# Quantised layer: maxima over partitions by a TensorE product; slot lists laid out by tile

## What is computed

```python
x = x + tanh(g_xattn[0]) * L0_xattn(layernorm(x), ctx)      # linear mix with the mean of the context
x = x + tanh(g_ffn[0])   * L0_ffn(layernorm(x))             # quantised layer
x = x + tanh(g_xattn[1]) * L1_xattn(layernorm(x), ctx)
x = x + tanh(g_ffn[1])   * L1_ffn(layernorm(x))             # 8 experts, the best two of each token
x = x + ...                                                  # layers 2 and 3
```

```python
def act_qdq(x):
    scale = max(max(abs(x)) / 32767, 1e-12)
    return clip(round(x / scale), -32768, 32767) * scale
x = act_qdq(x); up = act_qdq(x @ Wup.T); gate = act_qdq(x @ Wgate.T)
gate = act_qdq(gate * round_u16(sigmoid(gate)))
out = act_qdq(gate * up) @ Wdown.T
```

## Time and profile before

| | us |
|---|---|
| median of 3 runs | 1646.64 |
| lowest, highest | 1642.23, 1647.51 |
| profiled execution, its own time | 1650.74 |
| its span (first to last instruction) | 1649.0 |
| busy: PE, DVE, POOL, ACT | 1249.0, 1018.0, 857.6, 785.8 |
| mean granted TensorE clock | 0.878 |

### The profile page before, as it was taken

One profiled execution on the slowest core, in us unless ns is written; L12 is line 12 of the kernel. 1 busy time (PEld: TensorE's weight loads), 2 busy tenths in 40 slices (PEclk: granted clock), 3 DMA queues, 4 the chain that ended last, 5 costly groups with the idle time before them and its releaser, 6 DMA issues. The chain is left out here.

```text
span 1649.0 us, 27008 instructions
## 1 busy us (share of the span) xinstructions
PE 1249.0 (76%) x9879; PEld 859.6 (52%) x9880; DVE 1018.0 (62%) x2196; ACT 785.8 (48%) x1473; POOL 857.6 (52%) x1040
## 2 busy tenths in 40 slices
PE   4482658999547999565999958679998684999994
PEld 4231535555426899354555525545555553566663
DVE  5589748998461111354899967768886488544421
ACT  2277436777413444254667746556666341222220
POOL 5200046666305553584555549656665343588875
PEclk9696879999757999786899979889999597899997
DMA  2000000000025887110000000000000003344442
GB/s 100 7 0 0 1 2 2 2 2 1 4 58 165 246 228 201 48 52 21 1 2 2 2 15 1 1 3 2 2 1 1 11 31 127 75 97 97 98 87 24
DMA packets 51796, 74.96 MB, mean 45 GB/s; under 512 B 8169, under 2 KB 31602, under 8 KB 51282
## 3 DMA queue, kind: packets, MB, share of 16 engines
q1 hardware_dynamic: 35858, 55.01, 10.5%
q0 software_dynamic: 15808, 18.24, 6.7%
HBM read 57.09 MB, written 16.12 MB: 44 GB/s over the span
## 5 line engine op out<-in xcount | busy, mean ns | idle before, releaser
L1506 PE MATMUL ps<-topk_up_sb,topk_wu 128*128 128x512 f32 x256 | 118.7, 608 | 0.7 <-ACT topk_up_sb L1400 0.7
L500 POOL TENSOR_TENSOR l3x_prob<-l3x_prob,l3x_rden 128x1232 f32<-128x1232 f32 x32 | 71.9, 2248 | 78.3 <-DVE l3x_rden L633 78.3
L500 POOL TENSOR_TENSOR l2x_prob<-l2x_prob,l2x_rden 128x1232 f32<-128x1232 f32 x32 | 71.9, 2248 | 74.7 <-DVE l2x_rden L633 74.7
L1330 POOL DMA_INDIRECT out<-topk_shared,l3f_route_slots x64 | 100.2, 1565 | 17.5 <-issue 17.5
L1407 ACT ACTIVATE topk_ga<-ps 128x512 f32<-128x512 f32 x64 | 38.3, 598 | 148.0 <-PE ps L1506 148.0
L594 ACT ACTIVATE l3x_pt<-ps 77x512 f32<-77x512 f32 x128 | 72.5, 591 | 71.4 <-PE ps L544 71.4
L1626 DVE TENSOR_TENSOR sb_xnT<-topk_ga,ps 128x512 f32<-128x512 f32 x64 | 44.0, 687 | 97.8 <-ACT topk_ga L1407 97.8
L500 POOL TENSOR_TENSOR l1x_prob<-l1x_prob,l1x_rden 128x1232 f32<-128x1232 f32 x32 | 71.9, 2248 | 57.6 <-DVE l1x_rden L633 57.6
L1980 DVE TENSOR_TENSOR l1f_g_y<-ps,l1f_g_wd 128x256 f32<-128x256 f32 x39 | 16.6, 425 | 137.6 <-PE ps L1923 137.6
L1950 ACT ACTIVATE l1f_g_h<-ps,l1f_g_wd 128x256 f32<-128x256 f32 x156 | 63.5, 475 | 74.2 <-DMA l1f_g_wd<-l1f_W 41.0
L594 ACT ACTIVATE l2x_pt<-ps 77x512 f32<-77x512 f32 x128 | 72.7, 591 | 55.0 <-PE ps L544 55.0
(11 more groups left out here) (499 smaller groups left out, 3490.9 us busy)
## 6 DMA issues: line engine op xcount, KB each, us to landing
l1f_g_wd<-l1f_W SPq DMA_DIRECT2D x39, 322.0 KB, 4.0
l1f_g_wu<-l1f_W SPq DMA_DIRECT2D x39, 256.0 KB, 3.8
topk_wu<-l3f_W SPq DMA_DIRECT2D x16, 512.0 KB, 3.8
l1f_y_rows<-l1f_g_y SPq DMA_DIRECT2D x39, 128.0 KB, 4.0
topk_wd<-l3f_W SPq DMA_DIRECT2D x16, 256.0 KB, 2.7
l3f_rows<-l3f_route_own_rows SPq DMA_DIRECT2D x1, 2304.0 KB, 8.0
sb_x<-x SPq DMA_DIRECT2D x1, 2048.0 KB, 7.5
l1f_rows<-l1f_route_own_rows SPq DMA_DIRECT2D x1, 2048.0 KB, 9.2
```

The lines of the kernel that those rows point to most:

```text
L500: pool.tensor_tensor(prob[n % 4][:], prob[n % 4][:], rden[n % 2][:].unsqueeze(2).broadcast_to([P, HEADS, KEYS]), ALU.mult).then_inc(normed, 1)
L1330: pool.indirect_dma_start(out=out_rows, out_offset=spot(g, i), in_=y[g % 2][:, i, :], in_offset=None, compute_op=ALU.add).then_inc(y_added ...
L1506: ins = pe.matmul(ps[:, 2 * (c % 2) + i, :], wu[g % W][:, (i * CX + c) * P:(i * CX + c + 1) * P], xgT[g % 2][:], start=True, stop=True)
```

## The change

1. GpSimd no longer exchanges maxima. TensorE multiplies the column own maximum, spread over 128 columns as weights, with the identity: row by row the result in bank 6 is the list of all 128 partitions' maxima. VectorE's new `highest` reduces these 128 numbers from PSUM (semaphore found). The exchange run on `magic` goes too.
2. In slot_lists the tables hi_hot, hi_num, hi_table are laid out [P, CH, NHI], tile first. The tile number gets a full table (tile_table) and hi a spread copy (hi_wide[p]), both written by ScalarE, and hi_16 goes. The six instructions for the experts stand behind high(1).

```diff
@@ -722,13 +724,18 @@
 
+            def highest(k, n):
+                v.wait_ge(all_max, n)
+                v.tensor_reduce(col(k, 1), ps[:, 6, 0:P], X, ALU.max).then_inc(found, 1)
+                v.wait_ge(found, n)
+
             def own_scale(k, n):
-                v.wait_ge(all_max, n)
+                highest(k, n)
                 step(v.tensor_scalar(col(k, 2), col(k, 1), 1.0 / QMAX, 1e-12, ALU.mult, ALU.max))
...
             def product_scale(k, n):
-                v.wait_ge(all_max, n)
+                highest(k, n)
                 step(v.tensor_scalar(col(k, 2), col(k, 1), col(k, 5), 1e-12, ALU.mult, ALU.max))
@@ -839,20 +846,9 @@
         def _(pool):
-            def everywhere(k, n):
-                pool.wait_ge(own_max, n)
-                pool.partition_all_reduce(col(k, 1), col(k, 0), P, RMAX).then_inc(all_max, 1)
-
             pool.memset(magic[:], -MAGIC).then_inc(magic_ready, 1)
-            pool.wait_ge(magic_ready, 1)
-            pool.partition_all_reduce(qs[:, 31:32], magic[:], P, RMAX).then_inc(warm, 1)
             for b in range(NBLK):
                 norm.centre(pool, "pool", b)
-            everywhere(XS, 1)
-            everywhere(GATE, 2)
-            everywhere(UP, 3)
-            everywhere(H, 4)
-            everywhere(O, 5)
 
@@ -927,6 +923,13 @@
 
+            def everywhere(k, n):
+                pe.wait_ge(own_max, n)
+                if n >= 2:
+                    pe.wait_ge(found, n - 1)
+                pe.matmul(ps[:, 6, 0:P], col(k, 0).broadcast_to([P, P]), t["ident"][:], start=True, stop=True).then_inc(all_max, 1)
+
+            everywhere(XS, 1)
             for j in range(NBLK):
@@ -938,7 +941,12 @@
                 product(0, j).then_inc(up_made, 1)
+                if j == 0:
+                    everywhere(GATE, 2)
+            everywhere(UP, 3)
+            everywhere(H, 4)
             pe.wait_ge(loads, 32)
+            pe.wait_ge(found, 4)
             for b in range(NBLK):
@@ -950,6 +958,8 @@
                 ins.then_inc(vl_made, 1)
+            pe.wait_ge(kl_kept, NK)
+            everywhere(O, 5)
             for b in range(NBLK):
@@ -1694,8 +1704,9 @@
         lo_table, lo_16 = sb("lo_table", [P, P, CH], BF16), sb("lo_16", [P, NC * CH], BF16)
-        hi_hot, hi_num = [sb(f"hi_hot{p}", [P, NHI, CH], BF16) for p in range(2)], [sb(f"hi_num{p}", [P, 2, NHI, CH], BF16) for p in range(2)]
-        hi_table, hi_16, tile_16 = sb("hi_table", [P, NHI, CH], BF16), sb("hi_16", [P, NC * CH], BF16), sb("tile_16", [P, CH], BF16)
+        hi_hot, hi_num = [sb(f"hi_hot{p}", [P, CH, NHI], BF16) for p in range(2)], [sb(f"hi_num{p}", [P, CH, 2, NHI], BF16) for p in range(2)]
+        hi_table, tile_table = sb("hi_table", [P, CH, NHI], BF16), sb("tile_table", [P, CH, NHI], BF16)
+        hi_wide, hi_spread, hi_found = [sb(f"hi_wide{p}", [P, CH, NHI], BF16) for p in range(2)], s.one("hi_spread"), s.one("hi_found")
         nums = sb("nums", [P, NG * G, 2])
@@ -1743,8 +1754,11 @@
             sc.wait_ge(iotas, 6)
-            sc.activation(hi_table[:], iota_hi[:].unsqueeze(2).broadcast_to([P, NHI, CH]), ACT.Copy).then_inc(table_ready, 1)
-            sc.activation(tile_16[:], tile[:], ACT.Copy).then_inc(table_ready, 1)
+            sc.activation(hi_table[:], iota_hi[:].unsqueeze(1).broadcast_to([P, CH, NHI]), ACT.Copy).then_inc(table_ready, 1)
+            sc.activation(tile_table[:], tile[:].unsqueeze(2).broadcast_to([P, CH, NHI]), ACT.Copy).then_inc(table_ready, 1)
+            for p in range(2):
+                sc.wait_ge(hi_found, 1)
+                sc.activation(hi_wide[p][:], hi[:, p * CH:(p + 1) * CH].unsqueeze(2).broadcast_to([P, CH, NHI]), ACT.Copy).then_inc(hi_spread, 1)
             take(0, 1)
@@ -1756,7 +1770,7 @@
                 for i in range(CH):
-                    ins = pe.matmul(ps[:, 4, 0:2 * NHI], lo_hot[p][:, :, i], hi_num[p][:, :, :, i].rearrange("p k h -> p (k h)"),
+                    ins = pe.matmul(ps[:, 4, 0:2 * NHI], lo_hot[p][:, :, i], hi_num[p][:, i, :, :].rearrange("p k h -> p (k h)"),
                                     start=(p == 0 and i == 0), stop=(p == 1 and i == CH - 1))
@@ -1775,13 +1789,6 @@
                 step(v.tensor_tensor(first[:], first[:], groups[:], ALU.subtract))
-                step(v.memset(begun[:], 0.0))
-                step(v.tensor_tensor(begun[:, :, 0:E], iota_g[:].unsqueeze(2).broadcast_to([P, NG, E]),
-                                     first[:].unsqueeze(1).broadcast_to([P, NG, E]), ALU.is_ge))
-                step(v.tensor_tensor(u["of_expert"][:], begun[:, :, 0:E], begun[:, :, 1:E + 1], ALU.subtract))
-                step(v.tensor_tensor(begun[:, :, 0:E], u["of_expert"][:], iota_e[:].unsqueeze(1).broadcast_to([P, NG, E]), ALU.mult))
-                step(v.tensor_reduce(eid[:], begun[:, :, 0:E], X, ALU.add))
-                step(v.tensor_copy(u["expert_of"][:], eid[:]))
             step(v.tensor_tensor(flat(rank), flat(rank), ps[:, 2, 0:W], ALU.subtract))
@@ -1791,8 +1798,8 @@
             step(v.tensor_scalar(hi[:], lo[:], 1.0 / P, -0.5 + 0.5 / P, ALU.mult, ALU.add))
-            step(v.tensor_scalar(hi[:], hi[:], MAGIC, MAGIC, ALU.add, ALU.subtract))
-            step(v.tensor_copy(hi_16[:], hi[:]))
+            v.tensor_scalar(hi[:], hi[:], MAGIC, MAGIC, ALU.add, ALU.subtract).then_inc(hi_found, 1)
+            v.wait_ge(hi_found, 1)
             step(v.scalar_tensor_tensor(lo_16[:], hi[:], -float(P), lo[:], ALU.mult, ALU.add))
@@ -1801,14 +1808,22 @@
             def high(p):
-                step(v.tensor_tensor(hi_hot[p][:], hi_table[:], hi_16[:, p * CH:(p + 1) * CH].unsqueeze(1).broadcast_to([P, NHI, CH]), ALU.is_equal))
-                v.tensor_scalar(hi_num[p][:, 0, :, :], hi_hot[p][:], token[:], None, ALU.mult).then_inc(hi_ready, 1)
-                v.tensor_tensor(hi_num[p][:, 1, :, :], hi_hot[p][:], tile_16[:].unsqueeze(1).broadcast_to([P, NHI, CH]), ALU.mult).then_inc(hi_ready, 1)
+                v.wait_ge(hi_spread, p + 1)
+                step(v.tensor_tensor(hi_hot[p][:], hi_table[:], hi_wide[p][:], ALU.is_equal))
+                v.tensor_scalar(hi_num[p][:, :, 0, :], hi_hot[p][:], token[:], None, ALU.mult).then_inc(hi_ready, 1)
+                v.tensor_tensor(hi_num[p][:, :, 1, :], hi_hot[p][:], tile_table[:], ALU.mult).then_inc(hi_ready, 1)
 
...
             high(1)
+            step(v.memset(begun[:], 0.0))
+            step(v.tensor_tensor(begun[:, :, 0:E], iota_g[:].unsqueeze(2).broadcast_to([P, NG, E]),
+                                 first[:].unsqueeze(1).broadcast_to([P, NG, E]), ALU.is_ge))
+            step(v.tensor_tensor(u["of_expert"][:], begun[:, :, 0:E], begun[:, :, 1:E + 1], ALU.subtract))
+            step(v.tensor_tensor(begun[:, :, 0:E], u["of_expert"][:], iota_e[:].unsqueeze(1).broadcast_to([P, NG, E]), ALU.mult))
+            step(v.tensor_reduce(eid[:], begun[:, :, 0:E], X, ALU.add))
+            step(v.tensor_copy(u["expert_of"][:], eid[:]))
             v.wait_ge(taken[1], 1)
```

More of the change, by code:

```diff
@@ L675, in quantised_ffn @@
             s.one(n) for n in ("gate_made", "gate_kept", "up_made", "up_kept", "gate_q", "sig_made", "sig_whole"))
-        h_made, h_q, h_q_act, up_q, o_made, warm, o_raised, o_ready, down_made, residual, magic_ready, reduced = (
-            s.one(n) for n in ("h_made", "h_q", "h_q_act", "up_q", "o_made", "warm", "o_raised", "o_ready", "down_made", "residual", "magic_ready", "reduced"))
+        h_made, h_q, h_q_act, up_q, o_made, found, o_raised, o_ready, down_made, residual, magic_ready, reduced = (
+            s.one(n) for n in ("h_made", "h_q", "h_q_act", "up_q", "o_made", "found", "o_raised", "o_ready", "down_made", "residual", "magic_ready", "reduced"))
         ps, wraw, wT = t["ps"], t["l0f_wraw"], t["l0f_wT"]
```

## The result

| | before | changed |
|---|---|---|
| median | 1644.52 (4 runs) | 1623.70 (4 runs) |
| lowest, highest | 1642.23, 1647.51 | 1619.16, 1623.90 |
| profiled execution | 1650.74 | 1623.75, span 1621.7 |
| mean granted TensorE clock | 0.878 | 0.889 |

The account below looks back on a forecast made before the run. Barriers part the stages, so each one's path counts: late GpSimd in the opening, VectorE in the body, VectorE and TensorE alternating in slot lists. 8.7 + 0 + 2.25 + 10.2 = 21.2 us less than 1646.64: 1625.5, range 1619 to 1636.

Parts of the forecast that it names:

- Opening: Quantised layer's opening, centring: GpSimd follows VectorE's shifts without pause, own maximum at 63.3 in place of 72.05; 8.7 us less.
- Exchanges: Five exchanges of maxima in the quantised layer: x -2.28, gate +0.43, up +0.33, h and o +0.76 each.
- the 0 of the sum: Net of the five exchanges in the quantised layer: -2.28 + 2.28 = 0, bounds 1.5 us either way.
- TensorE's pause ahead of up product 1: Quantised layer: gate's exchange product delays up product 1 to about 103.6 from 101.6; costs nothing unless the clock falls.
- norm_project: Stage after the quantised layer: GpSimd starts at 219.25 in place of 221.50; 2.25 us less, bounds 1.9 and 2.6.
- Slot lists: Slot-list stage: expert work moved back, tile-first tables, contiguous moving operand; 10.2 us less, bounds 2.7 and 12.3.
- low(0): Slot-list stage: this VectorE table step starts at 471.5 in place of 474.08, 2.58 us earlier.
- product(1): End of slot-list stage: TensorE's second product starts at 483.4, takes 32 x 0.13 + 0.3, ends at 487.9.
- rival 3: Slot-list stage: TensorE's clock rises within product(1) once fed densely, saving 32 x 0.065; 1623.4 us, chance 0.08.
- Rival 4: Slot-list stage: VectorE loses its fast forms on the new shapes, 2.8 us each; 1634.8 us in all, chance 0.08.
- Rival 5: GpSimd: another instruction still calls for the exchange's load, so 8.7 and 2.25 fall away; 1636.5 us, chance 0.03.
- Rival 6: Attention stages: TensorE's clock granted low there, slower than before; 1652.5 us if low for 60 us, chance 0.02.

Follow-up runs that it names:

- e3: Kernel before without the exchange on magic in front, the other five exchanges still on GpSimd; median 1672.25 us, ratio 0.9946 to the kernel before.
- e2: Kernel before with the slot lists' part of the change alone; median 1667.41 us, ratio 0.9923 to the kernel before.
- e8: Changed kernel with 12 further 128x512 products on TensorE between the exchanges for up and for h; 1619.08 us in one run.
- e4: Changed kernel with high(1) made in two pieces of 16 tiles, the second product waiting for them in turn; median 1653.02 us, ratio 0.984 to the kernel before.
- e5: Changed kernel with 112 further products between the halves of slot_lists, moving elements and weights at various spacings; 1637.74 us in one run.
- e11: Changed kernel with slot_lists shortened, high(1) in pieces, tile table by GpSimd iota, first token product by ScalarE; median 1621.58 us, ratio 0.9849 to before.

## Why the prediction was right, point by point

- **Opening: -8.7 forecast, -8.68 measured** (own maximum 18.12 us into the stage, forecast 18.05). e3 shows the mechanism by itself.
- **Exchanges: up to o's maximum -0.76 forecast (the 0 of the sum, less o's own 0.76), -0.87 measured.** The own maxima stood at 72.05, 103.08, 141.99, 152.40 and 185.53 before, at 62.46, 91.13, 130.46, 141.19 and 175.07 now (x, gate, up, h, o). So gate to up takes 0.42 more (0.43 forecast), up to h 0.32 (0.33), h to o 0.75 (0.76). From x to gate it is 28.67 in place of 31.03, so -2.36 (-2.28 forecast). That this stretch fits to 0.1 is partly luck: it took 31.03, 31.74 and 32.55 in the three traces that keep x's exchange on GpSimd, and 28.58 to 29.10 in the ten that don't. At least part of this goes with the clock: 8 to 12 us behind x's own maximum it was granted at 0.94 in before and 0.57 in e2. The exchange alone, from own maximum to scale, went from 3.52 to 1.27, -2.25. TensorE's pause ahead of up product 1 shows nowhere: gate to up grew by gate's 0.42 alone.
- **Not in the forecast: 0.5 us from o's maximum to the stage's end.** This stretch grew by 1.29, not 0.76. TensorE's down products start at clock 0.50 in both kernels, but in the changed one the clock rises later behind them. That need not be the change's doing: in e2, whose quantised layer is that of before, it rises as late, and the stretch takes 29.73 in place of 29.10. The busy tables of before, the changed kernel and e2, from 2.6, 2.3 and 2.4 us behind the start of the down products (189.39, 179.69 and 191.08):

```profile
192.00:196.00 4.00, 4.00 (x33) 4.00 (x33) 1.68 (x2) 0.43 (x2) 0.00 (x0) 0.86 0.00 0
```
```profile
182.00:186.00 4.00, 4.00 (x27) 4.00 (x27) 1.04 (x2) 0.57 (x1) 0.00 (x0) 0.69 0.00 0
```
```profile
193.50:197.50 4.00, 4.00 (x27) 4.00 (x26) 1.05 (x2) 0.46 (x1) 0.00 (x0) 0.67 0.00 0
```

  What decides when it rises was not tried.
- **norm_project: -2.25 forecast, -2.47 measured.** GpSimd's first piece is 2.21 earlier in the stage.
- **Slot lists: -10.2 forecast, -10.70 measured** (to the last product 35.16 to 24.38 us behind the stage's start, -10.78). low(0) starts 2.53 earlier (2.58 forecast), high(1) ends 2.52 earlier, VectorE's forms kept their sizes, the first half ran at 0.13 a pair. The mis-sized term is product(1): 4.46 forecast, 3.83 measured. That is rival 3 in part, since the clock rose in its last 0.9 us; in e8 it rose before it, and the product took 2.41 at clock 1.00 (slot_lists 25.33). The last stage but one ahead of slot_lists, the same code in all, took 35.2 in e4 and 35.1 in e8 and 34.1 to 34.2 elsewhere; why is open. I had taken 18 us of strided products at clock 0.50 as evidence against a rise. e5 shows why that was no evidence: with TensorE's row full all the time, the clock stood at 0.50 under the contiguous first product, rose to 1.00 in the course of the first strided group, fell to 0.50 in the course of the third, and rose again under contiguous ones. So a full row of products, strided or not, doesn't tell by itself which clock is granted.
- **The rivals that are left.** Rival 4: VectorE's forms kept their sizes. Rival 5: no exchange and no "issue" is left on GpSimd. Rival 6: the attention of layer 1 took 0.29 less, not more.
- **The size against the median.** The four stages above the experts in the table gained 21.7 us, the medians 20.8. The profiled execution of before was 6.2 above its median; its extra lies in the experts (162.73) and other stages whose code is the same. Over all profiled kernels that stage took 159.2 to 162.7, so its -3.49 is not the change's.

## What to carry over

A GpSimd library instruction (here partition_all_reduce) costs a change twice, there (5.7 to 5.9 us) and back (7.0 to 7.4 in the opening), and "issue" in the profile with nothing in front of it is where to see it; a warming-up call pays only if no ordinary GpSimd work stands between it and its use. A largest value over partitions needs no such instruction: one product with the identity and a reduction of 128 elements take 0.9 to 1.3 us. That is more than the 0.49 of an exchange on GpSimd once it has nothing else to do; the gain came from the changes that went away, not from a faster exchange. To leave the last four exchanges on GpSimd would by these rows win some 2.3 us there and give some 2.2 back in the next stage, an estimate that no run tried. Lay bf16 operands so that the moving one has its neighbours in a row, or at most 8 bytes apart, let an idle engine write the repeated copy that keeps VectorE fast, and then cut the last table into pieces, so that TensorE starts on the first.

## What was not expected of the hardware

- The cost of a strided moving operand is a step, 0.146 at 8 bytes to 0.283 at 16, and is nearly the same at both clocks (0.28 at 0.50, 0.263 at 1.00).
- Weights 64 bytes apart cost nothing at either clock (0.13 and 0.068 a pair).
- The granted clock fell to 0.50 under strided products while TensorE's row was full.
- VectorE's instruction on 128x8 lasted 2.82 us beside a GpSimd iota; that had been only a rival of e11.
